# One-core attention chain: fp32 transposes in TensorE's transpose mode, probabilities transposed without an fp16 split

## What is computed

```python
# L0: w = weight[adapter_ids];  x = x + einsum('bsi,boi->bso', x, w)
# L1: 32 query heads, 8 key/value heads, head size 128, adapters of rank 16
q = lora_linear(x, wq, aq, bq, adapter_indices).reshape(B, Tt, H, D)
k = lora_linear(x, wk, ak, bk, adapter_indices).reshape(B, Tt, HKV, D)
v = lora_linear(x, wv, av, bv, adapter_indices).reshape(B, Tt, HKV, D)
q = apply_rope(q, positions, D, THETA)
k = apply_rope(k, positions, D, THETA)
...
logits = jnp.einsum('bqhgd,bkhd->bhgqk', qg, k) * scale
...
p = jax.nn.softmax(logits, axis=-1)
o = jnp.einsum('bhgqk,bkhd->bqhgd', p, v).reshape(B, Tt, H * D)
return lora_linear(o, wo, ao, bo, adapter_indices)
# L2: x = x + (x @ B_sel.T) @ A_sel.T
# L3: x = x + x @ W.T + b + 2 * (x @ A) @ Bm
```

## Time and profile before

| what | value |
|---|---|
| runs | 848.77, 849.9, 851.61 us |
| median | 849.9 us |
| span of the profiled execution | 850.1 us |
| TensorE busy | 797.7 us, 94% |
| VectorE busy | 621.6 us, 73% |
| ScalarE busy | 363.9 us, 43% |
| GpSimd busy | 307.9 us, 36% |
| mean granted TensorE clock | 0.978 |

### The profile page before, as it was taken

One profiled execution on the slowest core, in us unless ns is written; L12 is line 12 of the kernel. 1 busy time (PEld: TensorE's weight loads), 2 busy tenths in 40 slices (PEclk: granted clock), 3 DMA queues, 4 the chain that ended last, 5 costly groups with the idle time before them and its releaser, 6 DMA issues. The chain is left out here.

```text
span 850.1 us, 14916 instructions
## 1 busy us (share of the span) xinstructions
PE 797.7 (94%) x4780; PEld 674.6 (79%) x4780; DVE 621.6 (73%) x1556; ACT 363.9 (43%) x989; POOL 307.9 (36%) x261
## 2 busy tenths in 40 slices
PE   5699898999779999999999999999999999987898
PEld 5599786778568888888888888888888888865786
DVE  2568652488669789779779878878877977864783
ACT  3245442311054446446446446446445544543450
POOL 5300030044455336337336426435524632510220
PEclk9899999999989999999999999999999999999899
DMA  9992178887405123313304402602512211601302
GB/s 270 315 276 57 46 195 225 225 218 205 136 2 130 44 63 72 104 42 81 111 0 118 116 0 67 168 0 62 135 38 62 62 37 43 128 7 35 94 13 86
DMA packets 112750, 86.89 MB, mean 102 GB/s; under 512 B 60534, under 2 KB 79126, under 8 KB 112454
## 3 DMA queue, kind: packets, MB, share of 16 engines
q1 hardware_dynamic: 110770, 79.83, 35.7%
q0 software_dynamic: 1792, 6.49, 2.3%
q10 hardware_dynamic: 148, 0.07, 0.0%
HBM read 71.40 MB, written 20.73 MB: 108 GB/s over the span
## 5 line engine op out<-in xcount | busy, mean ns | idle before, releaser
L935 POOL TENSOR_TENSOR prob<-prob,rinv 128x512 f32<-128x512 f32 x64 | 66.7, 1042 | 198.6 <-DVE rinv L1025 198.6
L880 ACT ACTIVATE prob<-sm,nmax 128x128 f32<-128x128 f32 x256 | 99.8, 391 | 81.0 <-DVE nmax L1006 81.0
L928 POOL TENSOR_TENSOR qt<-qc,qs 128x512 f32<-128x512 f32 x60 | 96.0, 1599 | 94.8 <-DVE qs L964 94.8
L1102 PE MATMUL ps_out<-wo_hi,ot_hi 128*128 128x512 f32 x256 | 106.2, 415 | 5.4 <-DVE ot_lo L983 3.7
L1104 PE MATMUL ps_out<-wo_hi,ot_lo 128*128 128x512 f32 x256 | 100.6, 393 | 0.0
L82 PE MATMUL ps_q<-x1t_hi,blk_hi 128*128 128x512 f32 x240 | 100.5, 419 | 0.0
L1103 PE MATMUL ps_out<-wo_lo,ot_hi 128*128 128x512 f32 x256 | 99.6, 389 | 0.0
L1006 DVE CUSTOM_DVE_ANT_0 sm<-ps_s,maskbias 128x128 f32<-128x128 f32 x256 | 58.7, 284 | 53.8 <-issue 53.8
L83 PE MATMUL ps_q<-x1t_lo,blk_hi 128*128 128x512 f32 x240 | 95.5, 398 | 0.0
L84 PE MATMUL ps_q<-x1t_hi,blk_lo 128*128 128x512 f32 x240 | 95.2, 397 | 0.0
L964 DVE TENSOR_TENSOR qs<-ps_q,sin_t 64x512 f32<-64x512 f32 x120 | 82.6, 688 | 3.7
(11 more groups left out here) (207 smaller groups left out, 1937.1 us busy)
## 6 DMA issues: line engine op xcount, KB each, us to landing
wo_raw<-in_L_cond_wo SPq DMA_DIRECT2D x8, 1024.0 KB, 5.6
raw_w<-in_L_cond_wq SPq DMA_DIRECT2D x8, 1024.0 KB, 6.8
w_raw<-in_L_cond_weight SPq DMA_DIRECT2D x7, 1024.0 KB, 6.6
raw_b<-bq_sel SPq DMA_DIRECT2D x56, 128.0 KB, 4.6
raw_b<-bkv_sel SPq DMA_DIRECT2D x16, 256.0 KB, 6.7
v_hi_d<-v_hi SPq DMA_DIRECT2D x16, 256.0 KB, 3.7
v_lo_d<-v_lo SPq DMA_DIRECT2D x16, 256.0 KB, 4.9
k_rot<-kr SPq DMA_DIRECT2D x16, 256.0 KB, 2.6
```

The lines of the kernel that those rows point to most:

```text
L880: e = act.activation(prob[i][:, h, :], sm[:, h, :], ACT.Exp, bias=nmax[i][:, h:h + 1], scale=-1.0, accum_out=rsum[i][:, h:h + 1])
L928: pool.tensor_tensor(qt[:, half, h, :], qc[:, :], qs[:, :], ALU.add).then_inc(q_done, 1)
L935: pool.tensor_tensor(prob[i][:, :, :], prob[i][:, :, :], rinv[i][:, :].unsqueeze(2).broadcast_to([P, G, T]), ALU.mult).then_inc(prob_done, 1)
L1102: pe.matmul(ps_out[:, :], ot_hi[:, q], wo_hi[:, h, :], start=(h == 0), stop=False)
```

## The change

Every fp32 transpose that was a matmul with the identity (lines 277, 298 and 1238) gets `is_transpose=True`. The probabilities are turned in the same way, straight from the fp32 `prob`: `p_hi`, `p_lo`, the scaling by 4096 and the fp16 identity are gone, with their semaphores. TensorE's `turn` now waits for `prob_done`, which GpSimd gives; ScalarE's exponential waits for `t_ready` in place of `p_lo_done` before it writes a `prob` buffer again. `turn_ax` (fp32r) and the accumulating fp32 matmul at line 1284 stay as they were.

```diff
--- before.py
+++ after.py
@@ -25,7 +24,6 @@
 THETA = 500000.0
 HEAD_DIM = 128
 R_PACK = 16
-P_SCALE = 4096.0
 LORA_SCALE = 2.0
 
 
@@ -274,7 +271,7 @@
                                 pe.wait_ge(tile_lo_done, m - 2)
                             for n in range(KC):
                                 src = res[:, b, n * P:(n + 1) * P] if j == 0 else w0_raw[b % 2][:, n, (j - 1) * P:j * P]
-                                mm = pe.matmul(ps_ring[m % 3][:, n * P:(n + 1) * P], src, ident[:, :], start=True, stop=True)
+                                mm = pe.matmul(ps_ring[m % 3][:, n * P:(n + 1) * P], src, ident[:, :], start=True, stop=True, is_transpose=True)
                             mm.then_inc(tile_ready, 1)
 
                     def product(b):
@@ -295,7 +292,7 @@
                         if b >= 1:
                             pe.wait_ge(x1t_lo_done, b)
                         for k in range(KC):
-                            mm = pe.matmul(ps_x1[:, k, :], res[:, b, k * P:(k + 1) * P], ident[:, :], start=True, stop=True)
+                            mm = pe.matmul(ps_x1[:, k, :], res[:, b, k * P:(k + 1) * P], ident[:, :], start=True, stop=True, is_transpose=True)
                         mm.then_inc(x1t_ready, 1)
 
                     def adapters(b):
@@ -314,7 +311,7 @@
                     def turn_ax(b):
                         pe.wait_ge(axn_done, 4 * b + 4)
                         if b == 0:
-                            pe.wait_ge(ident_ready, 2)
+                            pe.wait_ge(ident_ready, 1)
                         else:
                             pe.wait_ge(axt_done, 3 * b)
                         for n in range(3):
@@ -368,7 +365,6 @@
                         act.dma_start(id_rows[:, n, :], ids.rearrange("(a b) -> a b", a=1)).then_inc(ids_in, 16)
                     act.wait_ge(consts_in, 16)
                     act.activation(ident_r[:, :], ident[:, :], ACT.Copy).then_inc(ident_ready, 1)
-                    act.activation(ident_h[:, :], ident[:, :], ACT.Copy).then_inc(ident_ready, 1)
                     split(0)
                     for b in range(B + 3):
                         if b + 1 < B:
@@ -734,9 +730,6 @@
             rsum = [sb(c, f"rsum{i}", [P, G]) for i in range(2)]
             rinv = [sb(c, f"rinv{i}", [P, G]) for i in range(2)]
             prob = [sb(c, f"prob{i}", [P, G, T]) for i in range(2)]
-            rsum_low = sb(c, "rsum_low", [P, G])
-            p_hi = sb(c, "p_hi", [P, G, T], F16)
-            p_lo = sb(c, "p_lo", [P, G, T], F16)
             pt_hi = sb(c, "pt_hi", [P, G * T], F32R)
             pt_lo = sb(c, "pt_lo", [P, G * T], F32R)
             ot_hi = sb(c, "ot_hi", [P, G * T], F32R)
@@ -866,7 +856,7 @@
                         act.wait_ge(o_ready, t + 1)
                         if i is None or i >= 1:
                             act.wait_ge(out_ready, t)
-                        act.activation(ot_hi[:, :], ps_o[:, :], ACT.Copy, scale=1.0 / P_SCALE).then_inc(ot_hi_done, 1)
+                        act.activation(ot_hi[:, :], ps_o[:, :], ACT.Copy).then_inc(ot_hi_done, 1)
 
                     def slots(g, first, last):
                         for b in range(B):
@@ -874,7 +864,7 @@
                             number = t if first else None
                             act.wait_ge(max_done, t + 1)
                             if not first or b >= 2:
-                                act.wait_ge(p_lo_done, t - 1)
+                                act.wait_ge(t_ready, t - 1)
                             i = b % 2
                             for h in range(G):
                                 e = act.activation(prob[i][:, h, :], sm[:, h, :], ACT.Exp, bias=nmax[i][:, h:h + 1], scale=-1.0,
@@ -980,7 +966,7 @@
 
                     def ot(t):
                         dve.wait_ge(ot_hi_done, t + 1)
-                        dve.scalar_tensor_tensor(ot_lo[:, :], ps_o[:, :], 1.0 / P_SCALE, ot_hi[:, :].bitcast(F32), ALU.mult, ALU.subtract).then_inc(ot_lo_done, 1)
+                        dve.tensor_tensor(ot_lo[:, :], ps_o[:, :], ot_hi[:, :].bitcast(F32), ALU.subtract).then_inc(ot_lo_done, 1)
 
                     def add(t, b):
 
@@ -1016,13 +1002,9 @@
                             if not last and b % 2:
                                 bq_lo_part(PAIRS * g + b // 2 + 1, b // 2)
                             dve.wait_ge(exp_done, t + 1)
-                            if not first or b >= 1:
-                                dve.wait_ge(inv_done, t)
                             if not first or b >= 2:
                                 dve.wait_ge(prob_done, t - 1)
-                            dve.tensor_scalar(rsum_low[:, :], rsum[i][:, :], 1.0 / P_SCALE, None, ALU.mult).then_inc(sum_done, 1)
-                            dve.wait_ge(sum_done, t + 1)
-                            dve.reciprocal(rinv[i][:, :], rsum_low[:, :]).then_inc(inv_done, 1)
+                            dve.reciprocal(rinv[i][:, :], rsum[i][:, :]).then_inc(inv_done, 1)
                             if not (last and b >= HALF):
 
                                 between = b % HALF != HALF - 1 and (not first or b >= 1)
@@ -1071,13 +1051,13 @@
                         mm.then_inc(s_ready, 1)
 
                     def turn(t, b):
-                        pe.wait_ge(p_lo_done, t + 1)
+                        i = b % 2
+                        pe.wait_ge(prob_done, t + 1)
                         if not isinstance(t, int) or t >= 1:
                             pe.wait_ge(pt_lo_done, t)
                         for h in range(G):
 
-                            pe.matmul(ps_t[:, h * T:(h + 1) * T], p_hi[:, h, :], ident_h[:, :], start=True, stop=False)
-                            mm = pe.matmul(ps_t[:, h * T:(h + 1) * T], p_lo[:, h, :], ident_h[:, :], start=False, stop=True)
+                            mm = pe.matmul(ps_t[:, h * T:(h + 1) * T], prob[i][:, h, :], ident[:, :], start=True, stop=True, is_transpose=True)
                         mm.then_inc(t_ready, 1)
 
                     def values(t, g, b):
@@ -1235,7 +1215,7 @@
                         if n >= 3:
                             pe.wait_ge(turn_lo_done, n - 2)
                         for k, tile in enumerate(tiles):
-                            mm = pe.matmul(ps_turn[n % 3][:, k * P:(k + 1) * P], tile, ident[:, :], start=True, stop=True)
+                            mm = pe.matmul(ps_turn[n % 3][:, k * P:(k + 1) * P], tile, ident[:, :], start=True, stop=True, is_transpose=True)
                         mm.then_inc(turn_ready, 1)
 
                     def wide(n):
```

More of the change, by code:

```diff
@@ L10 @@
 F32R = mybir.dt.float32r
-F16 = mybir.dt.float16
 I32 = mybir.dt.int32
@@ L93, in program @@
         ident_r = sb(whole, "ident_r", [P, P], F32R)
-        ident_h = sb(whole, "ident_h", [P, P], F16)
         axo = sb(whole, "axo", [2 * R, B, T])
@@ L764, in program @@
             exp_done = sem(c, "exp_done")
-            sum_done = sem(c, "sum_done")
             inv_done = sem(c, "inv_done")
             prob_done = sem(c, "prob_done")
-            p_hi_done = sem(c, "p_hi_done")
-            p_lo_done = sem(c, "p_lo_done")
             t_ready = sem(c, "t_ready")
@@ L892, in slots @@
                                 bq_hi_part(g + 1, p)
-                            act.wait_ge(prob_done, t + 1)
-                            if not first or b >= 1:
-                                act.wait_ge(t_ready, t)
-                            act.activation(p_hi[:, :, :], prob[i][:, :, :], ACT.Copy).then_inc(p_hi_done, 1)
                             if b == 1:
@@ L1033, in slots @@
                                 pt(t - 1)
-                            dve.wait_ge(p_hi_done, t + 1)
-                            dve.tensor_tensor(p_lo[:, :, :], prob[i][:, :, :], p_hi[:, :, :], ALU.subtract).then_inc(p_lo_done, 1)
                             if b == 1:
```

## The result

The changed kernel takes 830.7 us, the median of four runs (829.07 to 833.88), against 849.7 for the kernel before (four runs, one more than the three listed above): 19.0 us less by the medians. The ratio as measured is 0.976, 95% interval 0.973 to 0.979; the quotient of the two medians, 0.978, lies inside it. The forecast was 832.0. The profiled execution has a span of 832.2 us against 850.1, 17.9 us less. Executions more than 1.5% above the fastest of the same kernel are left out of medians and ratios: one of `outside_only` (851.1 us, the one that its trace is of) and one of `attention_only` (1125.2 us, at a granted clock of 0.65).

A forecast was written before the change was run, and what follows sets the result against it. TensorE was taken to bound the first stage's rounds and mid-attention, with VectorE next or other waits elsewhere. Terms -8, -2, -0.8, -3 and -4.3 sum to -18.1 us, from 850.1 to 832 us; range 816 to 848.

The forecast's parts named there:

- the last transposes of x1: End of the first stage: cheaper transposes of x1 there were to give 0.8 us.
- The price of a transpose: Everywhere on TensorE: 0.111 us each, paced by loading four-byte weights; bounds 0.057 and 0.222 us.
- First stage: Up to 106 us: cheaper transposes in the rounds were to give -8 us, between -5 and -10.
- The step for a round: First-stage round: from 9.81 to 8.3 us, 1.5 us less in each of four rounds, VectorE's 7.89 us just under.
- Steady attention: 250 to 738 us, 58 slots: 0.03 us saved a slot, -2 us (-5 to +1).
- Head of attention: Attention's first slots: less work in VectorE's queue brings the first product with the values forward by some 0.8 us.
- Late slots: Last four attention slots and drain: ot_lo 0.7 us earlier each without p_hi and p_lo, -3 us (-1.5 to -5).
- Last stage: Run of five tiles 2.6 us sooner, eight residual tiles 1.7: -4.3 us (-2.5 to -6).
- (1): Rival: the load in transpose mode is short, 0.057 us a transpose, mostly gaining in attention slots: 821 us; chance 0.22.
- (2): Rival: runs of transposes lower the clock in first-stage rounds and at the end, +10 us: 842 us; chance 0.09.
- (3): Rival: entering and leaving the mode drains the array, 0.32 us an attention slot: about 851 us, no change; chance 0.11.
- (4): Rival: one transpose takes 0.222 us, so attention slots pay 0.89 against 0.43 us: 873 us; chance 0.08.

The follow-up runs named there:

- outside_only: Kernel before, with transpose mode only in the three places outside attention; probabilities still split into fp16 halves: 840.5 us, ratio to before 0.988.
- attention_only: Changed kernel with the transposes outside attention back as fp32 products; only the probabilities turned in transpose mode: 842.0 us, ratio to before 0.990.
- outside_again: Kernel before with transpose mode only in the three places outside attention, run a second time for its trace: 841.9 us, ratio to before 0.989.
- copies_kept: Changed kernel with ScalarE's fp16 copy and VectorE's subtraction still carried out but not read by TensorE: 834.6 us, ratio to before 0.980.
- turn_twice: Changed kernel with the four transposes of each turn of probabilities carried out twice: 858.0 us, ratio to before 1.008.
- the probe: Changed kernel with unread work added at TensorE's end, including 120 transposes before and 120 after an idle time: 891.0 us.
- turn_as_product: Changed kernel without the flag on the probabilities' transposes, turned from fp32 by four plain products: 858.5 us, ratio to before 1.008.
- warm_all: Changed kernel with dummy products ahead of two first-stage waits for weights and also at that stage's end: 834.0 us, ratio to before 0.981.
- gathers_later: Changed kernel with GpSimd's 4 MB copies of bq and ao held until the sixth batch entry's tiles: 821.1 us, ratio 0.964.
- warm_waits: Changed kernel with dummy products ahead of two first-stage waits for weights: 834.6 us, ratio to before 0.981.

## Why the prediction was right

The forecast's case came out: the transpose costs what was forecast and each stage gained, though within the first stage one term, the last transposes of x1, did not come. That the sum lies 1.3 us from the median is luck in part, since the first stage gave less than forecast and steady attention more.

**The price of a transpose** (0.111 us) was right: 0.11 in the slot, 0.109 in a long run, 0.117 as a difference of whole slots. The reason given, that the load of four-byte weights sets the pace, is not shown: the stream of 128 columns sets it with half the load too.

**First stage** (-8): -5.3. The step for a round was sound, 8.3 us forecast and 7.99 measured, with VectorE in 7.60 of it. By rounds from the fourth entry on, before minus after: 1.1, 1.3, 1.8, 1.8, and 1.3 in the last up to its final product; 7.3 against the forecast's 7.3 for the same. The term for the last transposes of x1, -0.8, did not come: from the start of the last wide product to the second stage before takes 11.81 us (94.24 to 106.05) and the changed kernel 12.41 (88.35 to 100.76), 0.6 more. The clock explains it. In this stretch stand the adapters' twelve products of the last batch entry. Before has them almost wholly at the full clock; `attention_only`, with before's plain products for the transposes of this stage, has them at 0.50, and so has the changed kernel (windows in this order):

```profile
101.04:102.53 1.49, 1.49 (x12) 0.89 0.04 11
```
```profile
101.86:104.41 2.55, 2.55 (x13) 0.50 0.06 8
```
```profile
94.69:97.25 2.56, 2.56 (x13) 0.50 0.29 13
```

`attention_only` takes 12.86 us for the whole stretch, 1.05 more than before by these products alone. At the same low clock the changed kernel's 12.41 is 0.45 us less than that. So before's profiled execution was the faster of two, and the clock falls there without transpose mode as well.

The other 1.4 us is the arrival of the fourth entry's weights, taken as fixed. It is not: over two traces with products in that stage its mean is 41.05 us, over nine with transposes 41.07, but single ones lie from 38.7 to 42.7. So it looks like chance in this pair. First scores over the same traces come at 235.9 and 230.7 us, a gain of 5.2 (6.1 without the trace of `outside_only`, whose sixth entry's weights were late). The second stage, which has no transposes, adds its own scatter: 129.9 us in both of the pair, 127.9 to 132.8 over all traces.

**Steady attention** (-2): about -5.1, from the second to the sixtieth turn. The slot was forecast at 8.40 and is 8.37 or 8.38, against 8.43 or 8.44 in nearly all of before's; 0.06 over 57 slots is 3.4 us, and the second slot is 0.7 longer. The other 2.5 us were not in the forecast at all: every eighth slot of before, the first of a new head group, took 8.79 us, seven times in all, because TensorE stopped 0.35 us ahead of a product:

```profile
334.92 0.22 PE L1112 MATMUL ps_ao<-ot_lo,ao_pack 128*32 128x128 f32 x1
335.32 0.47 PE L1088 MATMUL ps_o<-pt_hi,v_hi 128*128 128x512 f32 x1 [0.18 <-issue]
```

The two other traces of kernels that keep the fp16 turn have the stop too, though not at every group (four times in `outside_only`, five in `outside_again`), and none that turns from fp32 has it, neither `copies_kept` nor `turn_twice` with its eight instructions. So it goes with the fp16 turn, not with the copies or the count of instructions; what it is stays open.

**Head of attention** (-0.8): -1.3, and it goes with the copies: from the first scores to the second turn the four traces with them take 19.0 to 19.5 us, the ten without 17.2 to 18.1. **Late slots** (-3): -2.0. The 0.7 us a slot was right (6.14 against 6.85), the number of slots was not: the last two distances between turns are 6.14 and 5.26 us in place of 6.85 and 6.84, the drain (from the last turn on) is 0.3 longer, and the two ahead of them, 7.2 and 6.14, are the same in both.

**Last stage** (-4.3): -4.2, of which 1.4 is the clock of before's profiled execution and 2.8 the change.

**The rivals.** (1) A load of 0.057 us: no, 0.11; the plain product's 0.222 us is halved, not quartered. (2) A falling clock: in the first stage it fell in stretches where before's had not, but its rounds kept 1.00 from 48 to 92 us, transposes alone brought it back in the probe, and holding it up through the waits gained nothing. (3) A cost of switching: none shows. (4) 0.222 us: that is the plain product, and `turn_as_product` shows the slower kernel it would have been, by 0.8% and not 2.7%, since the transposes elsewhere keep their gain in it (10 us) and its slots grew by 0.42 us, not 0.46.

**Left open:** whether and why the two kernels with dummy products are some 3 us slower than the changed kernel; the profiled execution of `warm_all`, 828.5 us, was the fastest of its six, with the first scores at 225.33 us and the weights of the fourth entry at 39.47. Whether the line of `gathers_later` would bring as much to the kernel before was not run.

## What to carry to other kernels

A 128x128 fp32 transpose in transpose mode costs half of the product with the identity, about as much as a pair of fp16 matmuls, so it pays where it replaces an fp32 product. In place of a split into fp16 pairs it gave little by itself here, 0.06 us of each 8.43 us slot; the rest of attention's 8.5 us came with the copies that were no longer needed and with the stops that went. Before counting a gain ahead of a wait for a transfer, look at what is queued ahead of that transfer: here one line that put 4 MB off brought 10 us, half of what the whole change had brought. Compare marks at the ends of stages over several traces, since one pair mixes the change with the arrival of a transfer (38.7 to 42.7 us here) and with a clock that was low in one of them (1.4 us in the last stage, 1.05 at the end of the first, 1.55 in `copies_kept`).

## What the runs showed of the hardware

The load record of a four-byte tile in transpose mode lasts 141 ns, against 192 for a plain product's, yet full loads follow each other no faster than every 0.11 us in either. A run of transposes alone brings TensorE from 1.2 to 2.4 GHz after an idle time, 5.5 us after its start, where products took 5.9. Faster work ahead of a wait makes the wait longer, and the clock behind it was more often low: after the wait that ends near 18 us, both traces with products there (waits of 0.95 and 1.93 us) have the clock at 1.00, and six of the nine with transposes (3.0 to 4.1 us) have it at 0.50. `warm_waits` kept it up and gained nothing by it; in its trace the next wait for weights is longer instead, 3.20 us.
